# Two self attentions of a decoder: another order of loads, of a round's first operations and of the key/value work

## The chip, the cores and the metric

The kernel runs as one launch on one core of one Trainium2 chip. The metric is the device time of a launch in microseconds (us); before the change it is 1560.36 us (median of 3 runs, 1557.02 to 1560.38). Instructions run on TensorE (PE, with weight loads as PEld), VectorE (DVE), ScalarE (ACT) and GpSimd (POOL), each in its own program order; almost all DMAs are issued by SyncE (SP), in order too.

## The reference, cut to what matters

A two-layer pre-norm decoder on x of shape (8, 256, 256): eight batches of 256 tokens, width 256, 16 heads of 16.

```python
x = x + _L0_attn_ref(_layernorm(x), wq, bq, wk, bk, wv, bv, wo, bo)   # causal, ALiBi bias, 16 key heads
x = x + _L0_xattn_ref(_layernorm(x), mask, ctx, ctx, ...)             # cross attention
x = x + _L0_ffn_ref(_layernorm(x), ...)                               # 8 experts, top 2
x = x + _L1_attn_ref(_layernorm(x), Wq, bq, Wk, bk, Wv, bv)           # causal, 4 key groups, no out projection
x = x + _L1_xattn_ref(_layernorm(x), ctx, ...)                        # cross attention with 8-bit rounding
x = x + _L1_ffn_ref(_layernorm(x), ...)                               # 16 experts, top 4, and a shared one

# in both self attentions
scores = einsum('bhqd,bhkd->bhqk', q, k) / sqrt(d)      # then causal mask
out = einsum('bhqk,bhkd->bhqd', softmax(scores), v)
```

The second layer's cross attention needs keys and values of the context, rounded to 8 bits: `kv = cond @ Wkv + bkv`, then a scale per head and `clip(round(k / s), -127, 127) * s`.

## The kernel before, in words

The kernel works through six stages in the order of the reference. The change is in the two self attentions (class `Attention`, L = 0 and 1), in the start of the program and in the work on the second layer's keys and values (`kv_tensor`, `kv_vector`, `kv_scalar`), which is done in small steps between operations of the second self attention.

**A batch in a self attention.** PE makes queries and keys of a batch (`pe_qk`, two halves, L219). To multiply float32 numbers with bf16 matmuls, ACT and DVE split each into three bf16 parts: `act_hi` (L619), `dve_res` (L520), `act_mid` (L627), `dve_lo` (L527). `sp_stack` writes the parts to DRAM (L733, L734, "wr") and loads them back as stacks of 102 or 96 rows (L743 for queries, L745 for keys, three DMAs each, "stack"). A DMA of it loads 48, 32 or 16 rows of 8 KB for 16 key heads; with 4 key groups the key rows are 2 KB. The loads of batch b wait for its writes, for the loads of batch b - 1 and for the last use of the buffer. There are three stack buffers.

**Two passes.** The first pass computes the scores with queries as rows (`pe_scores`, L409 and L412, 12 units a batch), and DVE takes their row maxima (`dve_max`, L540). The scores alternate between two PSUM banks, so unit u waits for the maximum of unit u - 2. `dve_np`, `pe_fold`, `act_mT` and `sp_max` (L751, "mrow") put the negated maxima into the query stack as three more rows. The second pass computes scores with keys as rows (`pe_attend_s`, L429 and L432), ACT takes the exponential (`act_exp`, L637), and PE multiplies with the values (`pe_attend_v`, L444 and L448). `act_out` (L643), `pe_fin1` (L457) and `dve_fin1` finish a batch.

**A round.** `tensor`, `vector` and `scalar` of `Attention` are written-out orders for the engines. Round i, from -2 to 8, makes queries and keys of batch i + 2, runs the first pass of batch i + 1 and the second pass of batch i, and finishes batch i - 1. A round on PE begins with

```python
if a: self.pe_qk(q, i + 2, 0); self.pe_qk(q, i + 2, 1)
if f: self.pe_attend_v(q, i - 1, 3)
if n: self.pe_v(q, i + 1); self.pe_scores(q, i + 1, 0); self.pe_scores(q, i + 1, 1)
```

(abridged), and the orders of DVE and ACT follow it. Each of the twelve steps u of a round ends with `steps(kv)` if b and u >= 3: one step of a generator beside the attention. In layer 0 it is `mix_tensor`, products of weights for the next stage; in layer 1 it is the key/value work of the fifth stage. What is left runs at the end.

**DMAs.** `sync_program` first issues the loads for layer 0 and the start of the next stage, then `Attention.sync`, which in round i issues `sp_stack(i + 2)`, from round 0 on one entry of a list of later loads, and `sp_max(i + 1)`. In layer 0 that list has six pieces of 1 MB of expert weights. SP waits where it stands for whatever a DMA needs.

Of the kernel before, what the change touches and what calls it, by code (L numbers as in the profile page):

```python
# [17 lines left out]
B, S, D, H, T = 8, 256, 256, 16, 16  # L18


class Signals:
# [23 lines left out]
    def landing(self, kind, *ix):  # L45

        return self.up(kind, *ix, by=16)
# [97 lines left out]
def decoder(nc, I, out):  # L145
    with ExitStack() as ctx:
# [76 lines left out]
        def x_ready(s, t):  # L223

            return [at("x", t // 4) if s == 0 and t < 4 else at(f"x{t // 4}", 0) if s == 0 else None,
                    at("x_a0", t) if s == 1 else None, at("x_c0", t) if s == 2 else None,
                    at("x_e", 0, t, 1) if s == 3 else None, at("x_a1", t) if s == 4 else None,
                    at("x_c1", t) if s == 5 else None]
# [99 lines left out]
        class Attention:  # L328
# [46 lines left out]
            def pt(self, b, g, kind):  # L375
                return self.PT[(12 * b + 3 * g + kind) % 6]

            def next_ln(self, i):

                return (self.ln, i + 3) if i + 3 < B else (self.ln + 1, i + 2 - B) if B - 2 <= i < B else None  # L380
# [91 lines left out]
            def tensor(self, q):  # L472
# [3 lines left out]
                for i in range(-2, B + 1):  # L476
                    a, n, b, f = i + 2 < B, 0 <= i + 1 < B, 0 <= i < B, i >= 1
                    if a:
                        self.pe_qk(q, i + 2, 0)
                        self.pe_qk(q, i + 2, 1)  # L480
                    if f:
                        self.pe_attend_v(q, i - 1, 3)
                    if n:
                        self.pe_v(q, i + 1)
                        self.pe_scores(q, i + 1, 0)
                        self.pe_scores(q, i + 1, 1)
                    if f:
                        self.pe_fin1(q, i - 1, 0)
                        self.pe_fin1(q, i - 1, 1)
                    if n:  # L490
                        self.pe_scores(q, i + 1, 2)
                        self.pe_scores(q, i + 1, 3)
                    for u in range(12):
# [10 lines left out]
                        if u == 7 and self.next_ln(i):  # L504
                            ln_turn(q, *self.next_ln(i), rp)
                        if b and u >= 3:
                            steps(kv)
                    if n:
# [58 lines left out]
            def vector(self, q):  # L567
# [9 lines left out]
                for i in range(-2, B + 1):  # L577
                    a, n, b, f = i + 2 < B, 0 <= i + 1 < B, 0 <= i < B, i >= 1
                    if a:
                        self.dve_res(q, i + 2, 0)  # L580
                        self.dve_res(q, i + 2, 1)
                        self.dve_lo(q, i + 2, 0)
                        self.dve_lo(q, i + 2, 1)
                    if n:
                        self.dve_v(q, i + 1)
                        self.dve_max(q, i + 1, 0)
                        self.dve_max(q, i + 1, 1)
# [3 lines left out]
                    if n:  # L591
                        self.dve_max(q, i + 1, 2)
                        self.dve_max(q, i + 1, 3)
                    for u in range(12):
# [12 lines left out]
                        if u == 8 and n:  # L607
                            self.dve_np(q, i + 1)
                        if b and u >= 3:
                            steps(kv)  # L610
                steps(kv, 999)
# [38 lines left out]
            def scalar(self, q):  # L650
# [3 lines left out]
                for i in range(-2, B + 1):  # L654
                    a, n, b, f = i + 2 < B, 0 <= i + 1 < B, 0 <= i < B, i >= 1
                    if a:
                        self.act_hi(q, i + 2, 0)
                        self.act_hi(q, i + 2, 1)
                        self.act_mid(q, i + 2, 0)
                        self.act_mid(q, i + 2, 1)  # L660
                    if f:
                        self.act_out(q, i - 1, 3)
                    for u in range(12):
                        if b:
# [5 lines left out]
                        if u == 8 and self.next_ln(i):  # L670
                            ln_copy(q, *self.next_ln(i))
                        if b and u >= 3:
                            steps(kv)
                    if n:
# [1183 lines left out]
        def sync_program(q):  # L1858
            e = q.e
            xd, od = I["x"].rearrange("(t p) d -> p t d", p=128), out.rearrange("(t p) d -> p t d", p=128)  # L1860
            e.dma_start(x[:, 0:4, :], xd[:, 0:4, :]).then_inc(*landing("x", 0))
            e.dma_start(W[:, 0:512], I["c_sq"]).then_inc(*landing("c", "sq"))
# [3 lines left out]
            attention[0].sp_rows(q)  # L1866
            for i in range(1, 4):
                e.dma_start(x[:, 4 * i:4 * i + 4, :], xd[:, 4 * i:4 * i + 4, :]).then_inc(*landing(f"x{i}", 0))
            e.dma_start(w_o0, rows_of("w_o0")).then_inc(*landing("w_o0", "w"))
            e.dma_start(b_o0, spread("b_o0")).then_inc(*landing("w_o0", "b"))  # L1870
            e.dma_start(w_xa, rows_of("w_xa0")).then_inc(*landing("w_xa", "w"))
            e.dma_start(ctxT[:, :, :], rows_of("ctxT")).then_inc(*landing("w_xa", "T"))
            e.dma_start(b_m0, spread("b_m0")).then_inc(*landing("w_xa", "m"))
            e.dma_start(w_r0, rows_of("w_r0")).then_inc(*landing("w_xa", "r"))
            q.wait_ge(at("consts", "z256"))
            for i, NE in enumerate((8, 16)):
                e.dma_start(XS[NE * RS:NE * RS + 128, :], zt256).then_inc(*landing("dummy", i))
            win_d, c0 = rows_of("w_in0"), 2048

            def win_piece(k, c):  # L1880
                return lambda: e.dma_start(win0[:, k, c:c + c0], win_d[:, k, c:c + c0]).then_inc(*landing("w_m0", k, c))

            q.wait_ge(at("consts", "all"))
            attention[0].sync(q, [win_piece(0, c) for c in range(0, 8192, c0)] + [win_piece(1, c) for c in range(0, 4096, c0)])
            q.wait_ge(*ends(1))
# [14 lines left out]

            def late(dst, src, *name):
                return lambda: e.dma_start(dst, src).then_inc(*landing(*name))

            attention[1].sync(q, [
                late(ws13, rows_of("ws13"), "w_m1", "s"),
                late(ws2, I["ws2"].rearrange("(c p) n -> p c n", p=128), "w_m1", "t"),
                late(w_r1, rows_of("w_r1"), "w_m1r", "r"),
                late(we2.rearrange("p (c n) -> p c n", c=16), I["we2"].rearrange("(c p) n -> p c n", p=128), "w_m1", "2")])
            q.wait_ge(*ends(4), at("kv_Vq"), at("kv_q"), at("kv_kM", 3, 1))
# [102 lines left out]
```

## Time and profile before

| what | value |
|---|---|
| median of 3 runs | 1560.36 us (1557.02 to 1560.38) |
| the profiled execution's own time | 1567.52 us |
| its span | 1565.4 us |
| mean granted TensorE clock | 0.887 |
| PE busy | 1210.1 us, 77% |
| DVE busy | 910.4 us, 58% |
| ACT busy | 677.5 us, 43% |
| first self attention | 0 to about 260 us |
| second self attention | about 617 to 862 us |

All rows come from one profiled execution. Times count from the start of its span. A busy PE is not PE at its peak. The granted clock is a share of 2.4 GHz: 1.00 is that level, 0.50 is 1.2 GHz.

### The profile page before, as it was taken

How to read it: one execution, taken by the hardware profiler on the slowest of the kernel's cores; microseconds unless marked ns; L12 is line 12 of the kernel's file. 1: busy time of each engine (PE TensorE's matmuls, PEld its weight loads, DVE VectorE, ACT ScalarE, POOL GpSimd, SP SyncE). 2: the span in 40 equal slices, each digit the busy share in tenths (PEclk: the TensorE clock that was granted, in tenths of full speed). 3: DMA queues.
4: the chain of work that ended last, by engine and by line, in shares of the span. 5: the costliest groups of instructions: out<-in, count | busy, mean ns of one | idle time of the engine just before them, and what ended most of it. 6: DMA issues, size and time to landing. Idle time of an engine off the chain costs nothing.

```text
span 1565.4 us, 25780 instructions
## 1 busy us (share of the span) xinstructions
PE 1210.1 (77%) x8255; PEld 826.6 (53%) x8255; DVE 910.4 (58%) x2570; ACT 677.5 (43%) x1412; POOL 398.6 (25%) x634
## 2 busy tenths in 40 slices
PE   4689988982999998478888657665766667999983
PEld 3367666771566665345565434443543444777642
DVE  3456554663223222467776889888888863644444
ACT  2144534330211211134445789778877862333200
POOL 1010101356100000412201335434543441000365
PEclk8699999995999999579999699779788868999997
DMA  8355532212111111634530200000000003444333
GB/s 218 92 138 132 134 94 102 75 48 84 38 48 44 44 48 53 154 88 97 129 77 3 108 1 28 28 11 18 29 28 10 20 27 105 144 151 149 115 110 111
DMA packets 82014, 122.58 MB, mean 78 GB/s; under 512 B 12454, under 2 KB 69926, under 8 KB 78383
## 3 DMA queue, kind: packets, MB, share of 16 engines
q1 hardware_dynamic: 72668, 95.77, 21.9%
q0 software_dynamic: 9216, 25.18, 5.4%
q8 instruction: 69, 1.13, 0.3%
q14 instruction: 61, 0.50, 0.1%
HBM read 76.73 MB, written 43.78 MB: 77 GB/s over the span
## 4 chain that ended last, share of the span: by engine, by line
PE 45%; issue 15%; ACT 12%; DVE 10%; DMA 7%; POOL 6%; SPq 3%; another core or an unknown queue 1%; POOLq 0%; ACTq 0%; DVEq 0%
PE ps L1039 12%; PE ps L219 12%; ACT work L1755 6%; PE ps L1056 6%; DMA W<-k_parts 4%; ACT work L1762 3%; PE ps L409 2%; PE ps L429 2%; DVE work L540 2%; POOL xs_scratch L1344 2%; PE ps L1024 2%; POOL work L1791 2%; PE ps L1048 2%; PE ps L444 1%
## 5 line engine op out<-in xcount | busy, mean ns | idle before, releaser
L1039 PE MATMUL ps<-W,work 128*128 x628 | 225.5, 492 | 5.0 <-issue 4.9
L1755 ACT ACTIVATE work<-ps,work 128x512 f32<-128x512 f32 x256 | 203.5, 809 | 29.0 <-POOL work L1791 28.7
L1258 DVE TENSOR_TENSOR work<-work,ps 128x128 f32<-128x128 f32 (+1 forms) x118 | 49.7, 421 | 241.3 <-ACT work L1324 241.3
L1604 PE MATMUL ps<-SM,work 128*128 128x512 bf16 x256 | 114.3, 448 | 89.2 <-ACT work L1755 85.0
L1698 DVE TENSOR_REDUCE work<-ps 128x1 f32<-128x512 f32 x256 | 173.8, 679 | 7.0 <-PE ps L1604 6.6
L637 ACT ACTIVATE work<-ps 128x512 f32<-128x512 f32 x192 | 112.9, 601 | 143.9 <-PE ps L432 138.2
L540 DVE TENSOR_REDUCE work<-ps 128x2 f32<-128x512 f32 (+1 forms) x192 | 128.2, 686 | 48.8 <-PE ps L412 47.3
L1039 PEld LDWEIGHTS ps<-W,work 128*128 128x128 f32 x628 | 110.7, 191 | 70.8 <-issue 66.2
L252 POOL TENSOR_TENSOR rstd<-ve,half 128x1 f32<-128x1 f32 x96 | 53.2, 558 | 353.1 <-DVE ve L247 351.5
L1791 POOL TENSOR_SCALAR work<-work 128x1 f32<-128x1 f32 x256 | 98.1, 383 | 167.9 <-DVE work L1698 159.6
L1762 ACT COPY work<-ps 128x1024 bf16<-128x1024 bf16 x128 | 132.0, 1033 | 0.4 <-PE ps L1614 0.4
L409 PE MATMUL ps<-W 102*128 102x256 bf16 (+3 forms) x512 | 82.3, 267 | 56.1 <-DMA W<-k_parts 28.6
L1056 PE MATMUL ps<-W,work 128*128 x470 | 121.0, 380 | 0.0
L1703 DVE TENSOR_SCALAR work<-work 128x512 bf16<-128x512 f32 x256 | 110.4, 431 | 13.1 <-ACT work L1755 11.8
L1324 ACT ACTIVATE work<-ps 128x128 f32<-128x128 f32 (+1 forms) x118 | 45.4, 384 | 165.9 <-PE ps L1039 165.8
L1614 PE MATMUL ps<-idb,work 128*128 128x128 bf16 x1024 | 111.9, 240 | 0.0
L1369 POOL DMA_INDIRECT W<-ys_scratch,work x64 | 62.6, 978 | 193.3 <-DMA ys_scratch<-work 166.1
L278 ACT COPY xnT<-ps 128x512 f32<-128x512 f32 x48 | 28.1, 586 | 164.0 <-PE ps L272 164.0
L1604 PEld LDWEIGHTS ps<-SM,work 128*128 128x128 bf16 x256 | 27.2, 106 | 126.8 <-ACT work L1755 117.1
L219 PE MATMUL ps<-xnT,W 128*128 128x512 f32 (+1 forms) x224 | 89.9, 561 | 5.2 <-ACT work L1334 3.3
L1614 PEld LDWEIGHTS ps<-idb,work 128*128 128x128 bf16 x1024 | 79.1, 107 | 20.7 <-issue 9.1
L409 PEld LDWEIGHTS ps<-W 102*128 102x128 bf16 (+1 forms) x512 | 41.9, 105 | 86.6 <-DVE work L540 46.0
(246 smaller groups left out, 2384.6 us busy)
## 6 DMA issues: line engine op xcount, KB each, us to landing
work<-xs_scratch SPq DMA_DIRECT2D x118, 128.0 KB, 2.1
ys_scratch<-work SPq DMA_DIRECT2D x118, 128.0 KB, 1.9
q_parts<-work SPq DMA_DIRECT2D x48, 128.0 KB
W<-q_parts SPq DMA_DIRECT2D x16, 384.0 KB
W<-in_w_in SPq DMA_DIRECT2D x6, 1024.0 KB, 19.4
W<-q_parts SPq DMA_DIRECT2D x16, 256.0 KB
W<-in_w_out SPq DMA_DIRECT2D x1, 4096.0 KB, 20.0
W<-in_we SPq DMA_DIRECT2D x1, 4096.0 KB, 12.7
```

Source lines behind the costliest of these rows:

```text
L219: mm = q.e.matmul(out_, l, r, start=start and i == 0, stop=i == n - 1, skip_group_check=True)
L409: q.e.matmul(PS[bk][:, w * i:w * i + w], qs[0:NA, h, 128 * j:128 * j + 128], ks[0:NA, h // self.per, 0:w], start=i == 0, stop=False, skip_ ...
L540: q.e.tensor_reduce(self.m[:, j, h0:h0 + n], ov, AX, ALU.max).then_inc(*up("mx", L, b, u))
L637: q.e.activation(self.pt(b, g, kind), PS[banks.of["ps2", L, b, g, kind]][:, :], ACT.Exp, scale=0.25).then_inc(*up("exp", L, b, g, kind))
L1039: mm = q.e.matmul(PS[bks[c]][:, 0:N], self.XT[s % 2][:, k, :], w[:, k, bass.ds(regs[s] + 512 * c if c else regs[s], N)], start=k == 0, sto ...
L1056: mm = q.e.matmul(PS[bk][:, 0:256], self.UT[s % 2][:, 128 * c:128 * c + 128], w[:, bass.ds(regs[s] + 256 * c if c else regs[s], 256)], sta ...
L1604: q.e.matmul(PS[bk][:, :], self.q3T[t % 2][:, h // 2, :], kM[:, h, :], start=True, stop=True).then_inc(*up("c1_s", t, h))
L1614: mm = q.e.transpose(PB[bk][:, 512 * (h % 2) + 128 * c:512 * (h % 2) + 128 * c + 128], self.ei[(H * t + h) % 3][:, 128 * c:128 * c + 128], ...
L1698: q.e.tensor_reduce(self.mm[:, h:h + 1], PS[banks.of["c1_s", t, h]][:, :], AX, ALU.max).then_inc(*up("c1_mx", t, h))
L1755: q.e.activation(self.ee[n % 4], PS[banks.of["c1_s", t, h]][:, :], ACT.Exp, bias=self.nb[:, h:h + 1], scale=self.sq[t % 2][:, h:h + 1], ac ...
L1762: q.e.copy(self.aT[n % 2], PB[banks.of["c1_at", n]]).then_inc(*up("c1_aT", n))
L1791: q.e.tensor_scalar(self.nb[:, h:h + 1], self.mm[:, h:h + 1], self.nsq[t % 2][:, h:h + 1], LN255, ALU.mult, ALU.add).then_inc(*up("c1_nb", ...
```

## The change

The diff has four parts.

1. Start: x is loaded as tiles 0 to 1, 2 to 7 and 8 to 15. Tiles 8 to 15 and the weights of later steps move behind the stacks of layer 0, into the list of `sync`, whose entries are now lists and are taken from round -2 on. The pieces of expert weights go from rounds 0 to 5 to rounds 1 to 6.
2. A round's start: in rounds where batch i + 1 has its first pass and batch i its second (i = 0 to 6), its first score units stand first on PE and their maxima first on DVE, with the two halves of `pe_qk` and `dve_res` between them.
3. ACT copies the last output of batch i - 1 between the two halves of `act_mid`.
4. The key/value work of layer 1 starts in round -2 and takes two steps at a time in rounds -2 and -1 (`beside`). For layer 0 nothing changes there.

```diff
-            return [at("x", t // 4) if s == 0 and t < 4 else at(f"x{t // 4}", 0) if s == 0 else None,
+            return [at("x" if t < 2 else "x1" if t < 8 else "x2", 0) if s == 0 else None,
...
+            def beside(self, i, u, kv):
+
+                if u >= 3 and i >= (0 if self.L == 0 else -2):
+                    steps(kv, 2 if i < 0 else 1)
...
+                    if b and n:
+                        self.pe_scores(q, i + 1, 0)
+                        self.pe_scores(q, i + 1, 1)
                     if a:
                         self.pe_qk(q, i + 2, 0)
+                    if b and n:
+                        self.pe_scores(q, i + 1, 2)
+                    if a:
                         self.pe_qk(q, i + 2, 1)
                     if f:
                         self.pe_attend_v(q, i - 1, 3)
+                    if b and n:
+                        self.pe_scores(q, i + 1, 3)
                     if n:
                         self.pe_v(q, i + 1)
-                        self.pe_scores(q, i + 1, 0)
-                        self.pe_scores(q, i + 1, 1)
                     if f:
                         self.pe_fin1(q, i - 1, 0)
                         self.pe_fin1(q, i - 1, 1)
-                    if n:
-                        self.pe_scores(q, i + 1, 2)
-                        self.pe_scores(q, i + 1, 3)
+                    if not b and n:
+                        for u in range(4):
+                            self.pe_scores(q, i + 1, u)
...
-                        if b and u >= 3:
-                            steps(kv)
+                        self.beside(i, u, kv)
...
+                    if b and n:
+                        self.dve_max(q, i + 1, 0)
+                        self.dve_max(q, i + 1, 1)
                     if a:
                         self.dve_res(q, i + 2, 0)
+                    if b and n:
+                        self.dve_max(q, i + 1, 2)
+                    if a:
                         self.dve_res(q, i + 2, 1)
+                    if b and n:
+                        self.dve_max(q, i + 1, 3)
+                    if a:
                         self.dve_lo(q, i + 2, 0)
                         self.dve_lo(q, i + 2, 1)
...
                         self.act_mid(q, i + 2, 0)
-                        self.act_mid(q, i + 2, 1)
                     if f:
                         self.act_out(q, i - 1, 3)
+                    if a:
+                        self.act_mid(q, i + 2, 1)
...
                         self.sp_stack(q, i + 2)
-                    if i >= 0 and beside:
-                        beside.pop(0)()
+                    if beside:
+                        for load in beside.pop(0):
+                            load()
...
-            e.dma_start(x[:, 0:4, :], xd[:, 0:4, :]).then_inc(*landing("x", 0))
+            e.dma_start(x[:, 0:2, :], xd[:, 0:2, :]).then_inc(*landing("x", 0))
...
+            e.dma_start(x[:, 2:8, :], xd[:, 2:8, :]).then_inc(*landing("x1", 0))
...
+            attention[0].sync(q, [
+                [late(x[:, 8:16, :], xd[:, 8:16, :], "x2", 0)],
+                [late(w_o0, rows_of("w_o0"), "w_o0", "w"), late(b_o0, spread("b_o0"), "w_o0", "b"),
+                 late(w_xa, rows_of("w_xa0"), "w_xa", "w")],
+                [late(ctxT[:, :, :], rows_of("ctxT"), "w_xa", "T"), late(b_m0, spread("b_m0"), "w_xa", "m"),
+                 late(w_r0, rows_of("w_r0"), "w_xa", "r")] +
+                [late(XS[NE * RS:NE * RS + 128, :], zt256, "dummy", i) for i, NE in enumerate((8, 16))],
+                *[[w] for w in win]])
```

In layer 1 the list of `sync` gets two empty entries in front, so its loads stay in rounds 0 to 3.

## Rows read from the trace of the kernel before

**Rows 1.** The page: busy time by engine, and the chain that ended last.
```profile
PE 1210.1 (77%) x8255; PEld 826.6 (53%) x8255; DVE 910.4 (58%) x2570; ACT 677.5 (43%) x1412; POOL 398.6 (25%) x634
PE 45%; issue 15%; ACT 12%; DVE 10%; DMA 7%; POOL 6%; SPq 3%; another core or an unknown queue 1%; POOLq 0%; ACTq 0%; DVEq 0%
```
**Rows 2.** Windows, layer 0: PE, PEld, DVE, ACT, POOL busy, clock, DMA share, GB/s.
```profile
142.85:168.06 25.21, 23.95 (x213) 17.67 (x211) 15.82 (x37) 12.40 (x25) 2.48 (x4) 1.00 0.55 136
217.10:222.70 5.60, 0.00 (x0) 0.00 (x0) 0.69 (x1) 0.00 (x0) 0.00 (x0) 0.88 0.15 63
222.70:241.40 18.70, 18.27 (x166) 13.48 (x170) 12.74 (x30) 8.35 (x16) 2.48 (x4) 0.85 0.02 6
```
**Rows 3.** The chain of waits, layer 0: start, length, what.
```profile
32.33 17.22 DMA W<-k_parts
...
77.40 17.31 DMA W<-k_parts
...
205.24 17.49 DMA W<-k_parts
```
**Rows 4.** The timeline of SP's queue, layer 0: start, length, line, DMA, count.
```profile
29.42 1.25 SPq L743 DMA_DIRECT2D W<-q_parts  x3
...
51.52 1.25 SPq L743 DMA_DIRECT2D W<-q_parts  x3
...
150.37 0.45 SPq L734 DMA_DIRECT2D k_parts<-work  x1
152.21 1.25 SPq L743 DMA_DIRECT2D W<-q_parts  x3
...
202.41 1.25 SPq L743 DMA_DIRECT2D W<-q_parts  x3
```
**Rows 5.** The timeline of PE, layer 0: start, length, operation, idle before and releaser.
```profile
142.85 3.67 PE L219 MATMUL ps<-xnT,SM 128*128 128x256 f32 x16
...
149.07 0.39 PE L409 MATMUL ps<-W 102*128 102x128 bf16 x4
...
222.77 0.61 PE L409 MATMUL ps<-W 102*128 102x128 bf16 x4 [5.67 <-DMA W<-k_parts]
```
**Rows 6.** The timeline of DVE, layer 0.
```profile
19.68 1.46 DVE L527 TENSOR_TENSOR work<-aux,work 128x512 bf16<-128x512 f32 x2
...
145.70 0.88 DVE L520 SCALAR_TENSOR_TENSOR aux<-ps,SM,work 128x256 f32<-128x256 f32 x2 [6.69 <-ACT work L619]
...
148.22 1.46 DVE L527 TENSOR_TENSOR work<-aux,work 128x512 bf16<-128x512 f32 x2
```
**Rows 7.** Short windows of layer 0: a stack's last part, and PE's clock after a wait.
```profile
146.00:147.00 1.00, 1.00 (x15) 0.50 (x17) 0.58 (x2) 0.44 (x2) 0.00 (x0) 1.00 0.16 58
...
222.00:224.00 2.00, 1.23 (x9) 0.96 (x10) 0.16 (x1) 0.00 (x0) 0.00 (x0) 0.50 0.15 57
...
228.00:230.00 2.00, 2.00 (x20) 1.68 (x19) 1.79 (x3) 1.20 (x2) 0.00 (x0) 0.95 0.00 0
```
**Rows 8.** Windows of layer 1: the start, then rounds 2, 4 and 5.
```profile
649.00:660.00 11.00, 6.68 (x23) 5.06 (x22) 2.67 (x7) 2.82 (x6) 3.71 (x4) 0.66 0.82 176
...
730.30:754.40 24.10, 19.78 (x188) 14.06 (x187) 18.20 (x47) 11.00 (x21) 6.37 (x8) 0.93 0.40 85
...
778.60:804.90 26.30, 21.89 (x200) 15.02 (x198) 19.56 (x47) 11.49 (x22) 2.50 (x4) 0.94 0.25 60
804.90:824.70 19.80, 18.55 (x211) 13.20 (x200) 14.22 (x35) 10.97 (x22) 1.41 (x2) 1.00 0.33 77
```
**Rows 9.** The chain of waits at the start of layer 1.
```profile
651.50 8.53 DMA W<-k_parts
```
**Rows 10.** The timeline of SP's queue, layer 1, round 2: the last stack load.
```profile
740.60 1.97 SPq L745 DMA_DIRECT2D W<-k_parts  x3
```
**Rows 11.** DVE groups, 675 to 846 us: key/value work, costliest and cheapest of 21.
```profile
L1485 DVE COPY SM<-ps 64x1024 bf16<-64x1024 bf16 x8 | 5.5, 688 | 0.9 <-PE ps L1422 0.6
...
L1495 DVE RECIPROCAL ctxN<-ctxN 128x2 f32<-128x2 f32 x1 | 0.2, 155 | 0.0
```

More of the change, by code:

```diff
@@ L585, in vector @@
                         self.dve_v(q, i + 1)
-                        self.dve_max(q, i + 1, 0)
-                        self.dve_max(q, i + 1, 1)
                     if f:
@@ L590, in vector @@
                         self.dve_fin1(q, i - 1, 1)
-                    if n:
-                        self.dve_max(q, i + 1, 2)
-                        self.dve_max(q, i + 1, 3)
+                    if not b and n:
+                        for u in range(4):
+                            self.dve_max(q, i + 1, u)
                     for u in range(12):
@@ L608, in vector @@
                             self.dve_np(q, i + 1)
-                        if b and u >= 3:
-                            steps(kv)
+                        self.beside(i, u, kv)
                 steps(kv, 999)
@@ L671, in scalar @@
                             ln_copy(q, *self.next_ln(i))
-                        if b and u >= 3:
-                            steps(kv)
+                        self.beside(i, u, kv)
                     if n:
@@ L1860, in sync_program, with late @@
             xd, od = I["x"].rearrange("(t p) d -> p t d", p=128), out.rearrange("(t p) d -> p t d", p=128)
-            e.dma_start(x[:, 0:4, :], xd[:, 0:4, :]).then_inc(*landing("x", 0))
+            def late(dst, src, *name):
+                return lambda: e.dma_start(dst, src).then_inc(*landing(*name))
+            e.dma_start(x[:, 0:2, :], xd[:, 0:2, :]).then_inc(*landing("x", 0))
             e.dma_start(W[:, 0:512], I["c_sq"]).then_inc(*landing("c", "sq"))
@@ L1866, in sync_program @@
             attention[0].sp_rows(q)
[L1867 to L1877, printed above, removed]
-            win_d, c0 = rows_of("w_in0"), 2048
[L1880 to L1884, printed above, removed]
+            e.dma_start(x[:, 2:8, :], xd[:, 2:8, :]).then_inc(*landing("x1", 0))
+            q.wait_ge(at("consts", "all"))
+            win_d, c0 = rows_of("w_in0"), 2048
+            win = [late(win0[:, k, c:c + c0], win_d[:, k, c:c + c0], "w_m0", k, c) for k, n in ((0, 8192), (1, 4096)) for c in range(0, n, c0)]
+            attention[0].sync(q, [
[6 more added lines that the diff above has]
+                *[[w] for w in win]])
             q.wait_ge(*ends(1))
@@ L1899, in sync_program @@
             e.dma_start(bp1, spread("b_p1")).then_inc(*landing("w_cr1", "bp"))
[L1901 to L1908, printed above, removed]
+            attention[1].sync(q, [[], [],
+                [late(ws13, rows_of("ws13"), "w_m1", "s")],
+                [late(ws2, I["ws2"].rearrange("(c p) n -> p c n", p=128), "w_m1", "t")],
+                [late(w_r1, rows_of("w_r1"), "w_m1r", "r")],
+                [late(we2.rearrange("p (c n) -> p c n", c=16), I["we2"].rearrange("(c p) n -> p c n", p=128), "w_m1", "2")]])
             q.wait_ge(*ends(4), at("kv_Vq"), at("kv_q"), at("kv_kM", 3, 1))
```

## The prediction

> **What bounds the kernel now.** I read the page first. PE is busy 77% of the span and leads the chain that ended last with 45%, but 7% of that chain is DMA [rows 1]. An average over six stages prices no single stage, so I went to the two self attentions: windows by round, then the chain of waits, then the timelines of SP's queue and of PE. The windows say that a full round of layer 0 takes 25.2 us, of which PE is busy 23.95 [rows 2]. That looks like a stage bound by PE, with little for a new order to win. The chain adds the second limit. Three times in layer 0 it passes through a load of stacks, each with 17.2 to 17.5 us from its last issue to its landing [rows 3]. Counted from the first of the six issues it is 29.42 to 49.55 and 202.41 to 222.73, 20.1 and 20.3 us [rows 3, 4]. I use 20.2.
>
> So each batch has a loop outside PE: queries and keys, three parts, written, loaded back, first pass. Take the round that starts with `pe_qk` at 142.85 [rows 5]. The lo parts are ready at 148.22 + 1.46 = 149.68 [rows 6], the last part is issued at 150.37, the first stack load at 152.21 [rows 4]; with 20.2 us the stack has landed at about 172.4. The next round starts at 168.06 [rows 2]. The stack therefore lands some 4.3 us **after** the start of the round whose first pass reads it. Today this costs almost nothing. PE has `pe_qk` (3.7 us), the last `pe_attend_v` and `pe_v` to do first, and reaches the scores 6.2 us into a round (142.85 to 149.07) [rows 5]. Where the load is late, in round 6, PE waits 5.67 us [rows 5], with all engines but one short DVE operation idle [rows 2].
>
> **Part 2, the new start of a round, in layer 0.** It removes nothing. It moves two score units ahead of `pe_qk`, a third between its halves, and the fourth ahead of `pe_v`. PE is in order: unit 0 of batch i + 1 waits for its stack, and behind it now stand `pe_qk` of batch i + 2, the last `pe_attend_v`, `pe_v`, `pe_fin1` and the whole second pass of batch i. `pe_qk` starts the next stack's loop, so the loop closes. From the landing of one stack to that of the next:
> - two score units, 0.9 us, two halves of `pe_qk`, 3.5 us, and a unit of 0.45 us between them: the second half ends at 4.9 us;
> - `act_hi` to 5.8, `dve_res` to 6.6, `act_mid` 0, `act_out` (0.6 us, newly ahead) and `act_mid` 1 to 7.6, `dve_lo` 0 and 1 to 9.0 us. Today the same stretch takes 149.68 - 142.85 = 6.8 us [rows 5, 6]. It grows by 2.1 us, or by 1.3 (the PE part alone) if ACT's detour is hidden;
> - writing the lo parts and starting the loads: 152.21 - 149.68 = 2.5 us [rows 4, 6];
> - the loads, 20.2 us.
>
> The sum is 31.7 us, with PE at the higher clock. But PE needs only some 24 us of it, and waits for the rest. After the wait of 5.67 us its granted clock stood at 0.50 (the level of 1.2 GHz) from 222, and was at 0.95 in 228 to 230 [rows 5, 7]. A round with a wait of 7 us starts in the same way: two units, `pe_qk`'s first half and the third unit then take 1.7 + 3.0 + 0.85 us, and only the second half runs fast, 2.3 us more. I take **34.0 us**, with 31.7 as the lower end.
>
> The Trainium skill bears on the 20.2 us. The row shows the DMA engines at a share of 0.16 near the end of a load, 58 GB/s [rows 7], less than three of sixteen. "DMA: Bandwidth & Descriptors", section "Why a DMA increments its semaphore by 16 and not by 1", says that a DMA runs on the largest number of engines up to 16 that divides the slowest dimension of both its sides, and on the lowest-numbered ones. By it the loads with outer dimensions 3 and 2 use three and two engines, and an estimate by the page's 27 GiB/s for one engine gives the lowest two, with 528 KB each, 19 us. That is a rule against the change, since a quieter queue would not shorten the load; with 19 us for the 17.3 of the row the sum would grow by 1.7 us a round.
>
> **Part 1, the start.** The lo parts of batch 0 are ready at 21.1 us [rows 6], but the first load is issued at 29.42, since the writes queue behind more than 5 MB of loads. With over half of that moved away, 2.5 us are enough, so issue at 23.7 and landing at 43.9 instead of 49.55: 5.7 us gained. Batch 1's loads started 2.0 us after batch 0's landing (51.52) [rows 4]. They now start at 45.9 and land at about 65.5. The bounds are 64.5, as in a quiet queue, and 66.5, beside the output and cross weights. SP and POOL are not late with these weights: the first user of any is in round 1. Tiles 8 to 15 are first read in round 1 as well.
>
> Round 0 on PE starts at 62.6 today, and stack 1 lands about 70. Now it starts at 65.5 with the scores. From there six loops lead to stack 7: 65.5 + 6 x 34.0 = 269.5. Today it lands at 222.7 [rows 3]. That is 46.8 us later, and the start's gain is inside this number. After it comes the same work as today's 18.7 us window [rows 2] and the two last rounds, plus `pe_attend_v` and `pe_v`, which PE did ahead of the wait and now does behind it: 3 us. Layer 0: **+50 us**; with 31.7 a loop, 65.5 + 190.2 = 255.7, thus +36 us. If the loads take 1 us more each it is +56.
>
> **Parts 2 and 3 in layer 1.** The key stacks are a quarter as large, and a load has landed 8.5 us after its last issue [rows 9]. In round 2 the last load's issue ends at 742.6 [rows 10], so the stack lands about 750.7, 3.6 us ahead of the next round at 754.4 [rows 8]. Here the new start can work: DVE's maxima fill its wait for `act_hi`. But the loop is there as well: 750.7 - 730.3 + 2.1 = 22.5 us is the shortest round. Rounds 0 to 6 take 28.0, 26.7, 24.1, 24.2, 26.3, 19.8 and 20.3 us (rounds 2, 4 and 5 in [rows 8]), 169.4 together. I expect 26, 24.5, 23, 22.5, 22.5, 22.5 and 17.5, together 158.5: 10.9 us less. Round 5 gets longer, since it has no expert sums and today beats the loop.
>
> **Part 4, the key/value work.** It stays the same: 29.2 us on DVE in 21 groups [rows 11], in 63 steps. Today it fills rounds 0 to 6. Now 36 steps, some 14 us of DVE work, go to rounds -2 and -1 and the rest ends in round 2; that is already in the shorter rounds 3, 4 and 6 above. Rounds -2 and -1 pay. DVE is busy only 2.67 of the 11 us from 649 to 660 [rows 8], but its work on batch 1 and PE's `pe_qk` of batch 1 stand behind the steps, and each step of 0.2 to 0.7 us waits for the one before it, or for PE at the lower clock. I let 6 of the 14 us hide and charge 8; the bounds are 0 (everything in idle time) and 14. Layer 1: -10.9 + 8 = **-3 us**, bounds -12 and +6.
>
> **The sum.** +50 - 3 = +47 us. On the profiled execution's own time, 1567.5 us (2 us over its span), that is 1614.5. It stands 7.1 us above the median of the three runs, so I carry the difference over: 1560.4 + 47 = **1607 us**.
>
> **The rivals.**
> - *The loop closes, but PE keeps its clock*, or the loads are a little shorter. For it: most of the wait's cost to the clock rests on one wait. Against: the wait would be longer than that one. +36 - 6 = +30: 1590 us.
> - *The stacks are in time, and the kernel gets faster.* The place is unit 0 at each start of a round in layer 0, the price is PE's wait there. It decides at a load of 25.2 - 9.0 - 2.5 = 13.7 us: below it there is no wait. Then 5.7 us come from the start, the waits of round 6 (5.7) and round 1 (1.9) go, and up to 1.3 us of idle PE in each of five rounds: -18, with -4 in layer 1: 1538 us. For it: the loads of the start no longer crowd the queue. Against: every load on the chain took over 17 us from its last issue, in the crowded start and in the quiet round 6 alike [rows 3].
> - *The key/value steps hold up layer 1*: each waits for a slow PE, batch 1 comes late, and rounds 0 to 2 carry steps as before. +50 + 14: 1624 us.
> - *The two cancel*: a loop of some 26 us, as with parts that are written earlier than I think. About 1560 us.
>
> **How the numbers follow.** Forecast 0.56, kept clock 0.18, stacks in time 0.08, held-up layer 1 0.14, cancelling 0.04. What a measurement of this kernel can tell from no change is about 0.3%, 5 us. Slower by more: 0.88; within: 0.04; faster by more: 0.08. For the range I take the bounds together: +36 and -12 give 1584, less 1 us on each of seven loads 1577, and the small chance of the other cases lets me go to 1574. Upward, +56 and +6 give 1622, and a little of both rivals 1628.
>
> **What would show it.** Right: in layer 0 the first L409 of rounds 0 to 6 waits 5 to 10 us for the key stack each time, landings are 31 to 35 us apart, and the granted clock falls each time; stack 0 lands near 44; layer 0 ends near 310 rather than 260. Layer 1 has rounds of 22 to 24 us without such waits, and no key/value work after round 2. Wrong: a load of stacks that takes under 15 us, rounds of 25 us in layer 0, or a first L409 without a wait. If the loop is right and only PE's clock stays at 1.00, the size is off, by 14 us.

## The result: 3.6% slower

The changed kernel takes 1614.99 us (median of 4 runs, 1612.41 to 1616.15) and the kernel before 1559.19 us (4 runs, 1557.02 to 1560.38). The ratio is 1.0357, 95% interval 1.0338 to 1.0376: 55.8 us slower. The forecast was 1607 us, 47 us slower, in a range of 1574 to 1628.

The profiled execution took 1616.15 us, with a span of 1614.2. Of the page after, the busy times, the chain that ended last, and the group of the score matmuls of the self attentions:

```profile
PE 1220.4 (76%) x8255; PEld 836.9 (52%) x8255; DVE 910.9 (56%) x2570; ACT 677.4 (42%) x1412; POOL 398.5 (25%) x634
PE 43%; issue 14%; ACT 13%; DMA 12%; DVE 11%; POOL 5%; SPq 3%; ACTq 0%; POOLq 0%; DVEq 0%
L414 PE MATMUL ps<-W 102*128 102x256 bf16 (+3 forms) x512 | 85.9, 278 | 99.9 <-DMA W<-k_parts 74.3
```

No engine has more instructions than in [rows 1]. PE is busy 10 us longer with the same 8255 matmuls; the mean granted clock fell from 0.887 to 0.868. What changed is the chain: DMA went from 7% to 12% of it. PE's idle time in front of the scores went from 56.1 us (28.6 of it until a key stack landed) to 99.9 us (74.3).

**Where the time went.** I cut both profiled executions at the same DMA issues on SP: the last load of `w_in` after layer 0, the load of `w_att1`, the last load of the experts' weights behind layer 1, and the first of the sixteen stores that open the last stage (1294.80 before, 1354.15 after). The stages between these cuts differ by 0.1 and 0.5 us. In us:

| stage | before | after | difference | forecast |
|---|---|---|---|---|
| layer 0, from the start of the span | 262.1 | 314.4 | +52.3 | +50 |
| layer 1, start (until the maxima of batch 0 are fetched) | 54.8 | 68.7 | +13.9 | +8 (start) |
| layer 1, the rest | 185.9 | 178.4 | -7.5 | -10.9 (rest) |
| last stage | 270.6 | 260.0 | -10.6 | 0 |

The last row isn't the change: its instructions are the same. It took 258 to 261 us in the changed kernel and in every kernel of the later two sets of runs below (e5 to e12), among them e7, which holds no part of the change. It took 266 to 271 us in the profiles of the kernel before and of e1 to e4. In those five, ACT and DVE wait in this stage for a releaser that the profile calls "remote"; in the other nine there is no such wait. In the kernel before the chain that ended last puts 19.2 us from 1479.1 on down to "another core or an unknown queue", and no compute engine is busy from 1495.7 to 1498.1. What that releaser is stays open. The time of the kernel before also moved between the sets, from 1565.8 us to 1556.7 and 1556.3. This row is why the two profiled executions differ by only 48.6 us.

**Layer 0.** The timeline of PE after: the first score matmul of each batch that waits for its key stack, from stack 1 on, with the idle time before it in brackets.

```profile
66.56 0.61 PE L414 MATMUL ps<-W 102*128 102x128 bf16 x4 [11.25 <-DMA W<-k_parts]
100.14 0.61 PE L414 MATMUL ps<-W 102*128 102x128 bf16 x4 [10.67 <-DMA W<-k_parts]
136.33 0.61 PE L414 MATMUL ps<-W 102*128 102x128 bf16 x4 [5.82 <-DMA W<-k_parts]
169.99 0.61 PE L414 MATMUL ps<-W 102*128 102x128 bf16 x4 [6.45 <-DMA W<-k_parts]
202.76 0.61 PE L414 MATMUL ps<-W 102*128 102x128 bf16 x4 [6.43 <-DMA W<-k_parts]
237.00 0.61 PE L414 MATMUL ps<-W 102*128 102x128 bf16 x4 [9.06 <-DMA W<-k_parts]
273.52 0.61 PE L414 MATMUL ps<-W 102*128 102x128 bf16 x4 [12.02 <-DMA W<-k_parts]
```

Every round of layer 0 now opens with PE standing still, 61.7 us in seven rounds; [rows 5] has one such wait, of 5.67 us. From one row to the next is one turn of the loop that the forecast described: 33.6, 36.2, 33.7, 32.8, 34.2 and 36.5 us, on average 34.5. The chain of waits passes through a stack load in each of them, and the loads are about as long as in [rows 3], 17.0 to 18.1 us but for the last:

```profile
82.79 17.30 DMA W<-k_parts
111.99 3.76 DMA k_parts<-work
118.58 17.70 DMA W<-k_parts
...
185.71 17.00 DMA W<-k_parts
...
253.33 20.15 DMA W<-k_parts
```

One turn from inside, on SP's queue. Stack 3 landed at 169.99 (PE's row above):

```profile
181.07 0.43 SPq L750 DMA_DIRECT2D k_parts<-work  x1
182.89 1.25 SPq L759 DMA_DIRECT2D W<-q_parts  x3
```

Landing to first load is 12.9 us, first load to the next landing (202.76) is 19.9 us, 32.8 together. The two turns of 36 us have something more. In the one that ends at 136.33 the write of the last part took 3.76 us (above) rather than 1.8. In the turn ahead of it SP had stood still when issuing two stores behind the load in flight, and the rows of maxima (second line) stood behind them:

```profile
84.75 7.57 SPq L1880 DMA_DIRECT2D xs_scratch<-SM  x2
92.36 4.94 SPq L767 DMA_DIRECT2D W<-work  x3
```

That the hold led to the slow write isn't shown: e10 has the same hold (7.91 us) and a write of 1.81, and its turn at this place took 34.5 us. In e2, which has no such stores there, it took 31.9.

In the other turn the last stack load, the one of 20.15 us, shared the DMA engines with a second piece of the experts' weights, issued at 263.80; the other loads have one piece or less behind them. It was as long in the three kernels of the same loads that I looked at (20.29, 19.41 and 19.82 us in e1, e5 and e10), and not in e2 (18.07), which has no second piece there.

PE's clock falls in each wait: in the 2 us behind each of the seven it is granted at 0.50. Windows after, in the columns of [rows 2]: the first us of the work behind the wait of 10.67 us, a later window, then two full turns.

```profile
102.00:104.00 2.00, 2.00 (x7) 1.55 (x6) 0.69 (x1) 0.00 (x0) 0.00 (x0) 0.50 0.01 1
106.00:108.00 2.00, 2.00 (x13) 1.43 (x15) 1.47 (x3) 0.32 (x1) 0.00 (x0) 0.98 0.00 0
100.10:136.30 36.20, 29.85 (x222) 22.02 (x222) 15.86 (x37) 13.51 (x27) 2.48 (x4) 0.88 0.39 96
170.00:202.70 32.70, 25.79 (x210) 19.34 (x210) 15.77 (x37) 12.36 (x25) 2.48 (x4) 0.87 0.41 105
```

The clock is granted at 0.50 (1.2 GHz) when PE comes back, and at 0.98 (close to 2.4 GHz) 6 us later. These two turns hold 29.85 and 25.79 us of busy PE, against 23.95 in the full round of [rows 2], with about as many matmuls. By the loop, only the slow matmuls up to the second half of `pe_qk` make the turn longer; the others take time in which PE would wait.

**Layer 1.** Windows of its start and of the rest, first of the kernel before, then of the one after.

```profile
621.40:676.20 54.80, 24.92 (x92) 15.31 (x93) 25.54 (x64) 6.59 (x14) 23.96 (x32) 0.59 0.55 139
676.20:862.10 185.90, 155.46 (x1474) 106.66 (x1472) 130.83 (x323) 85.40 (x161) 30.50 (x42) 0.94 0.33 79
```

```profile
673.80:742.50 68.70, 35.34 (x134) 20.30 (x135) 38.47 (x98) 7.60 (x17) 23.61 (x32) 0.63 0.44 113
742.50:920.90 178.40, 149.54 (x1433) 104.29 (x1430) 118.80 (x290) 84.53 (x158) 31.16 (x42) 0.90 0.35 82
```

Read DVE, the third engine. 12.9 us of work moved into the start, and the start became 13.9 us longer; 12.0 us left the rest, and that became only 7.5 us shorter. Before, DVE is busy in less than half of the start, but here little or nothing was hidden. PE too has 10.4 us more of busy time in the start, at a mean granted clock of 0.63 (0.59 before). The timeline of PE there shows why:

```profile
703.27 0.62 PE L1432 MATMUL ps<-idf,W 128*128 128x128 f32 x2 [5.05 <-DVE W L1477]
704.38 1.08 PE L272 MATMUL ps<-idf,xn 128*128 128x128 f32 x4 [0.49 <-DVE xn L260]
707.94 1.04 PE L1439 MATMUL ps<-idb,W 128*128 128x128 bf16 x8 [2.48 <-DVE W L1498]
708.77 3.73 PE L219 MATMUL ps<-W,ctxT 128*128 128x512 f32 x4
713.28 0.69 PE L1432 MATMUL ps<-idf,W 128*128 128x128 f32 x2 [0.78 <-DVE W L1477]
713.76 2.77 PE L219 MATMUL ps<-xnT,W 128*128 128x256 f32 x6
```

The last row is `pe_qk` of batch 1, 40.0 us after the load of `w_att1`. Before, it came 29.2 us after it. In between stand the steps of the keys and values: PE waits for DVE's, and their four matmuls on `ctxT` take 3.73 us at the clock of a PE that has idled (the same four took 1.88 us in a busy stretch of the kernel before).

### The profile page after: what moved, and what is told of

Read it like the earlier page. It is cut to its first block, busy times and chain, and to the rows that moved or that the text cites. A ratio compares the mean times of both kernels' runs of the same rounds, so it can differ in the third digit from the quotient of the medians.

```text
span 1614.2 us, 25777 instructions
## 1 busy us (share of the span) xinstructions
PE 1220.4 (76%) x8255; PEld 836.9 (52%) x8255; DVE 910.9 (56%) x2570; ACT 677.4 (42%) x1412; POOL 398.5 (25%) x634
## 4 chain that ended last, share of the span: by engine, by line
PE 43%; issue 14%; ACT 13%; DMA 12%; DVE 11%; POOL 5%; SPq 3%; ACTq 0%; POOLq 0%; DVEq 0%
PE ps L219 14%; PE ps L1056 12%; DMA W<-k_parts 8%; ACT work L1772 7%; PE ps L1073 6%; ACT work L1779 3%; POOL xs_scratch L1361 2%; DVE work L550 2%; PE ps L1041 2%; PE ps L1065 2%; PE ps L414 1%; DMA k_parts<-work 1%; POOL rstd L252 1%; POOL work L1808 1%; DVE x L1306 1%
## 5 line engine op out<-in xcount | busy, mean ns | idle before, releaser
L414 PE MATMUL ps<-W 102*128 102x256 bf16 (+3 forms) x512 | 85.9, 278 | 99.9 <-DMA W<-k_parts 74.3
L1056 PEld LDWEIGHTS ps<-W,work 128*128 128x128 f32 x628 | 110.6, 191 | 69.0 <-issue 64.2
L1073 PEld LDWEIGHTS ps<-W,work 128*128 128x128 f32 x470 | 80.2, 190 | 12.1 <-issue 0.4
## 6 DMA issues: line engine op xcount, KB each, us to landing
W<-in_w_in SPq DMA_DIRECT2D x6, 1024.0 KB, 19.2
```

The source lines that it names most:

```text
L414: q.e.matmul(PS[bk][:, w * i:w * i + w], qs[0:NA, h, 128 * j:128 * j + 128], ks[0:NA, h // self.per, 0:w], start=i == 0, stop=False, skip_ ...
L1056: mm = q.e.matmul(PS[bks[c]][:, 0:N], self.XT[s % 2][:, k, :], w[:, k, bass.ds(regs[s] + 512 * c if c else regs[s], N)], start=k == 0, sto ...
L1073: mm = q.e.matmul(PS[bk][:, 0:256], self.UT[s % 2][:, 128 * c:128 * c + 128], w[:, bass.ds(regs[s] + 256 * c if c else regs[s], 256)], sta ...
```

## Experiments

Nearly all are the changed kernel with a part switched off, or the kernel before with a part switched on. "Layer 0 ends" and the times of layer 1 are read from the profiled execution at the same cuts as in the table. Kernels that share a layer 0 give a measure of their scatter: the changed kernel with layer 0's old order (e5) and part 1 alone (e1) ended it at 260.7 and at 265.8 us, e6 and e11 at 241.6 and at 245.6. Medians of different sets can't be compared directly, since the kernel before moved by 9 us between them, so each run is judged by its ratio to the kernel before in its own set; the expectations in us for e1 to e4 counted from 1559 where their set had 1565.8.

**e1: part 1 alone** (the new order of the loads).

```diff
- e.dma_start(x[:, 0:4, :], xd[:, 0:4, :])
+ e.dma_start(x[:, 0:2, :], xd[:, 0:2, :])
...
+ attention[0].sync(q, [[x 8..16], [w_o0, b_o0, w_xa], [ctxT, b_m0, w_r0, two stores], [piece], ...])   # the list in words
```

> The kernel before with part 1 alone (the loads in order of need). Theory (the loss is the closed loop of part 2 in layer 0): stack 0 lands near 43 us instead of 49.6, layer 0 ends 4 to 6 us earlier, 1553 to 1556 us. Rival (the moved loads, x tiles 8 to 15, weights and expert pieces one round later, get in the way of stacks and maxima rows): a loss of its own, 1565 us or more.

Measured: 1569.75 us, ratio 1.0027 (1.0009 to 1.0045); layer 0 ends at 265.8. So it gains nothing, and the 4 to 6 us of the theory didn't come. Stack 0 did land earlier, at 43.4 instead of 49.55. But the next batch's parts then sat behind stack 0's load on SP (first three lines), and the last part of batch 2, issued beside stack 1's load, took long to land (the chain of waits, last line):

```profile
32.35 6.68 SPq L767 DMA_DIRECT2D q_parts<-work  x1
39.08 1.28 SPq L768 DMA_DIRECT2D k_parts<-work  x1
...
48.08 1.25 SPq L777 DMA_DIRECT2D W<-q_parts  x3
```

```profile
66.60 8.11 DMA k_parts<-work
```

Issuing one DMA, mostly 0.3 to 0.5 us, held SP for 6.68 us. Stack 1's first load came at 48.08 instead of 51.52. The write of 8.11 us took 1.84 in the kernel before (72.75 to 74.59), where stack 1 had landed first. So stack 2's first load came at 74.72, where it was before (74.59), and the gain of 6 us is gone after two batches. At the other end, stack 7 had a second piece of the experts' weights beside it, took 20.29 us, and PE waited 8.41 us for it instead of 5.67.

**e2: parts 2 and 3 in layer 0 alone**, and **e3: in layer 1 alone**. A flag for each layer guards the new order; parts 1 and 4 are undone.

```diff
+ new = NEW[L]              # e2: (1, 0), e3: (0, 1)
- if b and n:
+ if new and b and n:
      self.pe_scores(q, i + 1, 0)
```

> The kernel before with parts 2 and 3 in layer 0 alone. Theory: each round of layer 0 waits for its stack, landings 33 to 36 us apart, layer 0 ends 52 + 6 = 58 us later since the start's gain is missing; 1612 to 1622 us, with the first score of rounds 0 to 6 waiting 5 to 11 us for the key stack. Rival (the loss needs the moved loads as well): within 10 us of the kernel before.

> The kernel before with parts 2 and 3 in layer 1 alone. Theory: stacks there land ahead of the next round, so DVE's wait at a round's start is filled: rounds of 24 to 27 us become 22.5 to 26, 5 to 10 us less, 1549 to 1554 us. Rival (the new order costs by itself, through the two PSUM banks and the later start of the queries and keys): no gain or a loss, 1559 us or more.

Measured, e2: 1620.09 us, ratio 1.0357 (1.0313 to 1.0401), and layer 0 ends at 311.8. Two things are told by that. This order by itself makes the whole loss, 54 us here, and it needs nothing of the other parts. Layer 0 ends 50 us later, less than the 58 expected, as fits a start that has no gain to lose (e1). The waits are those of the changed kernel, here in rounds 0 and 1; the shortest of layer 0 is 2.90 us:

```profile
71.34 0.61 PE L415 MATMUL ps<-W 102*128 102x128 bf16 x4 [8.89 <-DMA W<-k_parts]
104.75 0.61 PE L415 MATMUL ps<-W 102*128 102x128 bf16 x4 [10.29 <-DMA W<-k_parts]
```

Measured, e3: 1561.23 us, ratio 0.9962 (0.9939 to 0.9985). Layer 1 took 233.4 us instead of 240.6, all of it after the start. The same new order that costs 50 us in layer 0 gains in layer 1, where PE waits only once for a key stack behind the start, 0.8 us.

**e4: part 4 alone** (keys' and values' work from round -2 on).

```diff
- if b and u >= 3:
-     steps(kv)
+ self.beside(i, u, kv)
```

> The kernel before with part 4 alone (key/value work from round -2 on). Theory: the second self attention's first maxima rows come about 14 us later, as in the changed kernel, and rounds 3 to 6 are shorter by 2 to 3 us each with 3 to 4 us saved at the last key/value steps: a net 0 to +6 us, 1559 to 1565 us. Rival (the author's): the work fills idle time at the start, 1550 us or less.

Measured: 1572.21 us, ratio 1.0042 (1.0026 to 1.0058). Layer 1's start took 65.4 us (10.6 more), the rest 179.2 (6.7 less): layer 1 got 4.0 us longer. Part 4 costs time without any help of the new order. The first maxima come 10.6 us later, not 14.

**e5: the changed kernel with layer 0's old order** (`NEW = (0, 1)`).

> The changed kernel with layer 0's order of before: parts 1 and 4, and parts 2 and 3 in layer 1 alone. Theory (layer 0's closed loop is the whole loss): layer 0 ends near 266 us as with the loads alone, layer 1 takes 247 us as in the changed kernel instead of 241: 6 to 12 us above the kernel before on this chip, 45 to 50 us below the changed kernel. Rival (the parts only hurt together, for instance the loads with the key/value work): 20 us or more above the kernel before.

Measured: 1561.86 us, ratio 1.0037 (1.0017 to 1.0056). Only the order of layer 0 separates it from the changed kernel and its +55.8 us. The ratios of e1, e3 and e4 multiply to 1.0031, so nothing of the size of the loss comes from the parts meeting each other. An effect of some 5 us can't be excluded by that, and the stages show one: e3 and e4 change layer 1 by -7.2 and +4.0 us, and with both it took 245.1 (e5) and 247.1 us, 4.5 and 6.5 more than before.

**e6 and e7: the stack loads spread over all DMA engines**, in the changed kernel and in the kernel before. The same bytes, as DMAs whose slowest dimension is 48, 32 or 16 rows in the queries and 16 rows in the keys, instead of 3, 2 or 1 stacks. (Abridged: the semaphore calls are left out.)

```diff
- for k, (s, c, n) in enumerate(((0, 0, 3), (3, 0, 2), (5, 0, 1))):
-     q.e.dma_start(qs[16 * s:16 * s + 16 * n], rows(DQ, s, c, n, False))
- for k, (s, c, n) in enumerate(((0, 0, 3), (3, 1, 2), (5, 2, 1))):
-     q.e.dma_start(ks[16 * s:16 * s + 16 * n], rows(DK, s, c, n, True))
+ for k, (s, n) in enumerate(((0, 3), (3, 2), (5, 1))):
+     src = bass.AP(DQ.tensor, DQ[0].offset, [[4096, 16 * n], [1, 4096]])
+     q.e.dma_start(qs[16 * s:16 * s + 16 * n, :, :], src)
+ for s, c in enumerate((0, 0, 0, 1, 1, 2)):
+     q.e.dma_start(ks[16 * s:16 * s + 16, :, :], rows(DK, s, c, 1, True))
```

> The changed kernel with the same bytes of each stack load spread over all DMA engines: the query rows as one flat dimension of 48, 32 and 16 rows, the key rows as six loads of 16 rows instead of three of 48, 32 and 16 (nine load DMAs for six). Theory (a load takes 17 to 18 us because its slowest dimension of 3 or 2 keeps it on 3 or 2 engines): the loads land 8 to 11 us after the last issue, the loop of layer 0 falls below a round's work, the waits of 5 to 11 us go; 1550 to 1570 us. Rival (the load is slow because of the 8 KB rows, or because of what stands ahead and behind in the queue): landing stays over 15 us and the time within 10 us of the changed kernel, about 1615.

> The kernel before with the spread loads. Theory: it gains what it still waits for stacks, some 8 us for each of the first two, 5.7 in round 6 and 2 in round 1, less 1.2 us of extra issue a batch: 15 to 22 us less, 1544 to 1551 us. Rival (as above): no gain, 1560 us or more.

Measured, e6: 1536.46 us, ratio to the kernel before 0.9864 (0.9836 to 0.9892), so 4.8% under the changed kernel by the two ratios; layer 0 ends at 241.6. The time is below the 1550 to 1570 us expected. This is the test of the loop: nothing but the shape of the stack loads was changed (nine DMAs for six), and the loss is gone. The timeline of SP, then of PE:

```profile
64.37 1.25 SPq L778 DMA_DIRECT2D W<-q_parts  x3
65.66 3.00 SPq L780 DMA_DIRECT2D W<-k_parts  x6
...
70.16 0.94 SPq L1899 DMA_DIRECT2D xs_scratch<-SM  x2
```

```profile
76.69 0.61 PE L415 MATMUL ps<-W 102*128 102x128 bf16 x4 [2.83 <-DMA W<-k_parts]
```

A stack takes 12.3 us from first issue to landing, where it took 19.9. Two waits are left behind this one, of 0.32 and 1.11 us. The two stores that held SP for 7.57 us now take 0.94. The write that held SP for 6.68 us in e1 takes 0.34. The share of the DMA engines near the end of a load says why. First the changed kernel, whose stack landed at 100.14, then e6:

```profile
97.00:100.00 3.00, 0.00 (x0) 0.00 (x0) 0.00 (x0) 0.00 (x0) 0.00 (x0) 0.50 0.17 61
```

```profile
75.00:76.00 1.00, 0.00 (x0) 0.00 (x0) 0.00 (x0) 0.00 (x0) 0.00 (x0) 1.00 1.02 137
```

Under three of sixteen engines were busy while the narrow load came to its end, and all of them beside the spread one; that row has the load of `ctxT`, issued behind the stack, in flight as well. The rule of the Trainium skill that the prediction named, in "DMA: Bandwidth & Descriptors", section "Why a DMA increments its semaphore by 16 and not by 1", agrees with both rows.

Measured, e7: 1535.94 us, ratio 0.9867 (0.9839 to 0.9894); layer 0 ends at 246.4, layer 1 takes 235.2. With short loads the kernel before takes the same time as the changed one. It gains 21 us, 15.7 in layer 0 and 5.4 in layer 1; the 7% of DMA on its chain, some 110 us, is no measure of that.

**e8: the kernel before with spread loads and parts 2 and 3 in both layers.**

```diff
  (e7)
+ new = NEW[L]              # (1, 1)
```

> The kernel before with the spread loads and parts 2 and 3 in both layers, the loads at the start and the key/value work as before. Theory: with stacks in time, the new order no longer costs in layer 0 and keeps its 6 us in layer 1: equal to or up to 10 us below the spread kernel before, 1535 to 1548 us. Rival (the order costs in layer 0 even without a late stack, through PSUM banks and a later start of queries and keys): 10 us or more above the spread kernel before.

Measured: 1533.77 us, ratio 0.9859 (0.9828 to 0.9891); layer 0 ends at 244.8, layer 1 takes 234.0. Against e7 the new order gains 2 us by the medians, inside both intervals: harmless where the stack is in time, and worth next to nothing. The 7.2 us that it gained in layer 1 with the narrow loads (e3) are 1.2 here.

**e9: the changed kernel with only the keys' loads spread.**

```diff
- for k, (s, c, n) in enumerate(((0, 0, 3), (3, 1, 2), (5, 2, 1))):
-     q.e.dma_start(ks[16 * s:16 * s + 16 * n], rows(DK, s, c, n, True))
+ for s, c in enumerate((0, 0, 0, 1, 1, 2)):
+     q.e.dma_start(ks[16 * s:16 * s + 16, :, :], rows(DK, s, c, 1, True))
```

> The changed kernel with only the key rows' loads spread (six loads of 16 rows); the query rows stay on 3 and 2 engines. Theory (the most loaded engine sets the load): the busiest engines carry 312 KB a stack instead of 528, so a load takes 12 to 14 us from its first issue instead of 20.2, the loop of layer 0 is 24 to 27 us, and most of the loss goes: 1538 to 1560 us where the fully spread kernel had 1536. Rival (any DMA that stays narrow holds up the whole stack): landings near 17 us after the last issue and 1600 us or more.

Measured: 1538.21 us, ratio 0.9895 (0.9873 to 0.9916), layer 0 ends at 241.3. From the first issue (63.69) to the landing (76.01) it is 12.3 us, as with both spread:

```profile
67.57 8.44 DMA W<-k_parts
```

So it is enough to take the keys' bytes off the few engines, as the theory of the most loaded engine had it. Whether the queries' alone would do the same wasn't run.

**e10: the changed kernel without part 3** (`act_mid` 1 ahead of `act_out` again).

```diff
  self.act_mid(q, i + 2, 0)
+ self.act_mid(q, i + 2, 1)
  if f:
      self.act_out(q, i - 1, 3)
- if a:
-     self.act_mid(q, i + 2, 1)
```

> The changed kernel with part 3 undone: both halves of act_mid again ahead of the last output copy. Theory (the loop counts every step from landing to writing): the lo parts are ready 0.6 us earlier in each of six loops of layer 0, 3 to 4 us less than the changed kernel, ratio to the kernel before 1.031 to 1.035. Rival (the copy lies beside DVE's work and is hidden): no difference, within 2 us.

Measured: 1614.32 us, ratio 1.0377 (1.036 to 1.0395). Nothing came back, so the rival was right. A stack landed at 168.94 and the last part was issued at 180.71, 11.8 us later; with part 3 that was 169.99 to 181.07, 11.1 us. ACT's detour is hidden.

**e11: the versions put together**: spread loads, parts 1 to 3, the keys' and values' work where the kernel before has it. **e12: the same, with that work from round -1 on**, one step at a time, so nine steps early.

```diff
- if u >= 3 and 0 <= i < B:                              # e11
+ if u >= 3 and (0 if self.L == 0 else -1) <= i < B:     # e12
      steps(kv)
```

> The kernel before with the spread loads, the loads at the start in order of need and parts 2 and 3 in both layers; the key/value work stays as before. Theory: with the spread loads the start's gain is no longer eaten (layer 0 ends near 241 us instead of 245) and layer 1 keeps its start without the key/value work: 2 to 6 us below the spread kernels of the last call, ratio to the kernel before 0.980 to 0.985. Rival: the start's gain is lost again further on, 0.985 to 0.988.

> As the run before, with the key/value work started one round early instead of two and at one step at a time (9 steps instead of 36 in rounds -2 and -1). Theory (a step ahead of round 0 costs about 0.4 us each, 14 us for 36 steps, and gives 0.3 us back later): the first maxima rows of layer 1 come 3 to 5 us later than in the run before, and the time is within 3 us of it. Rival (only round -2 is the trouble, where PE waits between batch 0's and batch 1's queries): no delay and 3 us or more gained.

Measured, e11: 1533.56 us, ratio 0.9848 (0.9831 to 0.9865). Beside e8 (0.9859), it shows nothing for part 1: layer 0 ended at 245.6, and not near 241 as the theory had it (e8: 244.8).

Measured, e12: 1528.07 us, ratio 0.9816 (0.9799 to 0.9833), 28.3 us under the kernel before and the fastest of all. My theory of it failed: I had expected a start 3 to 5 us longer. The rival, no delay and 3 us or more gained, fits. The windows of its start and of the rest of layer 1:

```profile
605.20:658.20 53.00, 24.43 (x101) 15.71 (x102) 27.77 (x72) 6.95 (x15) 23.89 (x32) 0.69 0.57 146
658.20:835.80 177.60, 150.62 (x1464) 105.68 (x1462) 127.19 (x316) 85.02 (x160) 31.11 (x42) 0.94 0.34 82
```

The start is 0.6 us longer than e11's 52.4 and the rest 4.0 us shorter than its 181.6. What part 4 wanted can be had, in a quarter of the steps. That it is round -2 alone that costs, as the rival says, wasn't tested apart from the number of steps.

## Why the prediction was right, and where its sizes were off

**Right: the mechanism.** The step was "unit 0 of batch i + 1 waits for its stack, and behind it now stand `pe_qk` of batch i + 2 ... so the loop closes". e2 shows that this order alone makes the loss, e5 that without it the loss is gone, and e6 and e9 that it hangs on the length of the load. Of the signs that the forecast named, the waits were 5.8 to 12.0 us for 5 to 10, the landings 32.8 to 36.5 us apart for 31 to 35, and layer 0 ended at 314 for 310.

**Layer 0, +52.3 us for +50.**
- *The load, 20.2 us*: 19.9 in a quiet turn.
- *The rest of the turn, 13.8 us with the slow clock*: 12.9. ACT's detour of 0.8 us, taken for the likelier end, was not there (e10). The lower end of that bound, the PE part alone, was the true one.
- *The turn, 34.0 us*: 34.5 on average. The quiet turn of 32.8 is under the forecast. Two things that the sum left out lift the mean: SP held at two stores, and the last load beside a second piece of the experts' weights. e2, which has neither, has turns of 33.1 on average. I had the first in hand: part 1 moves those stores right behind a stack load, and I priced the move only as "beside the output and cross weights". How the stores lengthen the turn stays open (above). Six turns: 207.0 us instead of 204.0.
- *The start, landings at 43.9 and 65.5*: 41.6 and 66.5. The gain for stack 0 was real and larger than forecast. For stack 1 it was 1 us smaller than in the sum. Part of that is the sum's own: its terms, 45.9 + 20.2, give 66.1 and not 65.5. And the first load followed the landing of stack 0 by 4.6 us and not 2.0 (46.27 - 41.65), behind the held write (7.20 us here, as in e1).
- *After the last stack, 3 us more*: 40.9 against 39.4 us, so 1.5.

**Layer 1, +6.4 us for -3, at the upper bound of +6: the terms mis-sized.** The first is the step "I let 6 of the 14 us hide and charge 8". The start paid 13.9 us for 12.9 us of DVE's work here, and 10.6, 11.7 and 10.4 in e4, e5 and e10 with the same early steps. I had counted DVE's idle time, but in the start PE and DVE wait for each other in turn, and batch 1 stands behind the steps. The bound of 14 us held, and the value taken in it was too low. The second is the gain of the rounds, 7.5 us for 10.9. The steps and the new order share it: e3 alone gains 7.2 in layer 1, e4 alone 6.7 in the rest, and the two together 7.5 rather than 14. The first rounds after took 26.0, 24.4, 25.7, 23.1, 23.1 and 17.8 us; round 2 has 25.7 for the forecast's 23. The loop of the stacks isn't what stops them: in the rest PE waits once for a key stack, 1.7 us. In front of the scores it waits for DVE's maxima, 15.0 us there, 16.3 in the kernel before, 10.9 in e3 and 20.4 in e4. Why the two gains don't add, no run took apart.

**The sum.** Layers 0 and 1 together: +58.7 us in the profiles, +55.8 in the medians, +47 forecast. The profiles miss the forecast by 11.7 us, 9.4 in layer 1 and 2.3 in layer 0. The time lies as near to the rival of 1624 us as to the forecast of 1607.

**The rivals.**
- *PE keeps its clock*: wrong. The granted clock was 0.50 after each of the seven waits.
- *The stacks are in time*: wrong for this kernel, and right as a mechanism. It put the turning point at a load of 13.7 us and the time below it at 1538 us. e6 and e9 have loads of 12.3 us, and 1536.5 and 1538.2 us. That these meet the 1538 so closely is partly luck: short loads by themselves take the kernel before to 1535.9 us (e7).
- *The key/value steps hold up layer 1*: this is what happened there, with layer 1 at +6.4 us where the rival had +14.
- *The two cancel*: wrong, no turn was under 32.8 us.
- The rule of the Trainium skill on the number of DMA engines ("DMA: Bandwidth & Descriptors", the section named above) held (e6). The estimate from its rate, 19 us for a load after its last issue, did not: it is 17.0 to 18.1 us in all turns but the last. Counted from the first issue, 19.9 us, the load is near to it.

## What to carry to other kernels

Before work that waits for a transfer is moved to the head of an in-order engine's round, compare when the transfer lands with when the round starts, and look at what now stands behind the wait: if the next transfer's source is among it, slack becomes a closed loop whose length is every round's. Then look at the DMA share during the transfer. Here a share of 0.16 to 0.18 marked a transfer that could be made shorter by its shape, and that was worth 21 us in the kernel before (e7), more than every reordering tried. Side work moved into a prologue can cost nearly its full length, though the engine idles there: ask what that idle time waits for, and whether the side work delays it. A quarter of the steps cost some 0.6 us (e12), so its amount and place are worth a run.

## What the runs showed of the hardware

- A DMA's issue can hold the issuing queue: one write took 6.68 us on SP (e1; 7.20 in the changed kernel), two stores 7.57 us, each behind stack loads with few engines at work. With the loads spread, the write took 0.34 us and the two stores 0.94 (e6).
- A write can land late beside such a load: 128 KB issued at 66.60 took 8.11 us in e1, and 1.84 in the kernel before, where the load had landed.
- Spreading half of the bytes (the keys') shortened a load as much as spreading all: 19.9 to 12.3 us.
- The last stage, with unchanged instructions, took 266 to 271 us in five profiles and 258 to 261 in the nine others. Only the five have waits there for a releaser that the profile can't name.
